# Attention block on one core: projection jobs in halves over two slots, z double-buffered and in parts, the shift copied straight to its row

## The chip, the cores and the metric

The kernel runs on one core of a Trainium2 chip. The metric is the device time of one launch in microseconds, as the median of several runs.

## The reference

Group norm over a 4 x 256 x 32 x 32 input (32 groups), attention with 4 heads of 64 channels over the 1024 positions of each image, an output projection and the residual:

```python
x_n = _group_norm(x, gn_w, gn_b)
q = _conv1x1(x_n, wq, bq); k = _conv1x1(x_n, wk, bk); v = _conv1x1(x_n, wv, bv)
q, k, v = (to_heads(q), to_heads(k), to_heads(v))
attn = jnp.einsum('bhqd,bhkd->bhqk', q, k) * hd ** (-0.5)
attn = jax.nn.softmax(attn, axis=-1)
out = jnp.einsum('bhqk,bhkd->bhqd', attn, v)
out = out.transpose(0, 1, 3, 2).reshape(bsz, c, h, wd)
return x + _conv1x1(out, wp, bp)
```

## The kernel before, in words

Every float32 factor is split into a float16 high and low part, and three products stand for one. Channels lie on two tiles of 128 partitions (index t or i), positions on two halves of 512 (index j).

**Slots.** The work is a hand-written order of 128 slots, 32 per image: an image has 8 units (a head and a half of its queries), a unit 4 slots of 256 keys. `G` counts all slots, `g` those of the image. In slot G TensorE makes the scores of G (four matmuls of 512 columns into `st[G % 2]`, lines 551 and 552), two score maxima of a unit six slots ahead (`maximum`, 529, into the banks `mxb`) and the weighed values of slot G - 4 (`weigh`, 24 matmuls of 64 or 65 columns into the bank `pv`). ScalarE reads the scores twice (739: float16 `p_hi`, 742: the full value, back into `st` in even slots and into `p32` in odd ones). The low half `p_lo` is their difference, on VectorE in even slots (830) and on GpSimd in odd ones (1023). `st` is free for slot G + 2 when that is done.

**The shift.** The softmax subtracts an upper bound of each query's score. VectorE reduces each maxima tile (806), joins the partial maxima (`join_max`, 811) at the end of the slot with G % 4 = 1; TensorE transposes the four columns in the next slot (`shift_transpose`, 536, which takes a turn in the banks `mxb`), VectorE scales the four rows (`row_out`, 818) and SyncE copies them to row 64 of `q_max` (`shift_to_row`, 369), where the scores of the unit two slots on read them.

**Jobs.** `JOBS` names, by slot, whole projections of 128 channels x 512 positions into the one bank `gen`: k, q, v of this image's second tile (i = 1) or of the next image, y (the output projection) of the image before, and two group statistics (mean, var). A k, q or y job is six matmuls of 512 columns, a v job 24 of 128 (`job` and `parts`, 480). ScalarE evicts the bank in the same slot, GpSimd makes the high and low halves of k and q in the next (997, 330), VectorE the low half of v (824). SyncE then copies the halves to the layouts of the matmuls (`dup_all`: six copies for k, six for q, each for both halves).

**z.** The normalised input of the next image: VectorE takes channel statistics (847), TensorE averages over groups (517, 519), ScalarE evicts, GpSimd works out the factors (`about_group_mean`, `norm_factors`), ScalarE makes `xin` into z (758, slots 10 and 11) and `z_hi` (763, slots 13 and 14), GpSimd `z_lo` (316, slots 14 and 15).

**Normalise** (837, 838) divides a unit's weighed values when its last `weigh` is done; the next unit's first `weigh` waits for it.

Instructions run in order on each engine and in the DMA queue of SyncE.

Of the kernel before, what the change touches and what calls it, by code (L numbers as in the profile page):

```python
# [6 lines left out]
F16 = mybir.dt.float16  # L7
ALU = mybir.AluOpType
# [4 lines left out]
def attention_block(nc, x, gn_w, gn_b, wq, bq, wk, bk, wv, bv, wp, bp, out):  # L13
# [17 lines left out]
    MXJ = 2 * QT + 1  # L31
# [19 lines left out]
    JOBS = {0: ("k", 1, 1, 0), 1: ("y", 0, 0, -1), 2: ("q", 1, 1, 0), 3: ("y", 1, 0, -1), 4: ("mean", 0, 0, 1),  # L51
# [9 lines left out]
    FIRST_IMAGE = {4: ("v", 0, 1, 0), 6: ("mean", 0, 0, 1)}  # L61


    MAX_MIDWAY = ((), (), (), (2, 3), (6, 7), (MXJ - 1,))
# [6 lines left out]
    with ctx:  # L71
# [29 lines left out]
        eps = sb("eps", [P, CT])  # L101
        first_use = sb("first_use", [P, CT])
# [5 lines left out]
        z_hi = sb("z_hi", [P, CT, HW], F16)  # L108
        z_lo = sb("z_lo", [P, CT, HW], F16)
# [14 lines left out]
        shift_row = sb("shift_row", [QT, 2, P], F16)  # L124
# [43 lines left out]
        s_mv = sem("s_mv")  # L168
        s_gmean = sem("s_gmean")
# [6 lines left out]
        s_zlo = [sem(f"s_zlo{t}") for t in range(CT)]  # L176
# [15 lines left out]
        s_dup = {n: sem(f"s_dup_{n}") for n in "kq"}  # L192
        s_first = [sem(f"s_first{h}") for h in range(2)]
        s_first_q1 = sem("s_first_q1")

        s_mx_full = sem("s_mx_full")
        s_mx_free = sem("s_mx_free")
        s_shift = sem("s_shift")
# [37 lines left out]

        def nth(i, j, b):
            return 4 * b + 2 * i + j
# [16 lines left out]
        def long_at(G):  # L255
            todo = job_at(G)
            return todo is not None and todo[0] in LONG
# [17 lines left out]
        def wait_p_lo(eng, G):  # L275
            wait(eng, s_plo_dve if lo_on_dve(G) else s_plo_pool, G // 2 + 1 + (G == TOTAL - 1))
# [37 lines left out]
        def z_low(eng, b, t):  # L314
            wait(eng, s_zhi, CT * (b - 1) + t + 1)
            eng.tensor_tensor(z_lo[:, t, :], xin[:, t, :], z_hi[:, t, :], ALU.subtract).then_inc(s_zlo[t], 1)

        def wait_z(eng, b, j=1):

            if b == 0:  # L320
                wait(eng, s_z0_lo, CT * (j + 1))
            else:
                for t in range(CT):
                    wait(eng, s_zlo[t], b)
# [773 lines left out]
```

## Time and profile before

| | us |
|---|---|
| median of 3 runs | 397.02 (396.8 to 398.1) |
| profiled execution | 398.07 |
| its span | 396.2 |
| TensorE busy | 368.2 (93%) |
| ScalarE busy | 304.6 (77%) |
| VectorE busy | 303.2 (77%) |
| GpSimd busy | 258.9 (65%) |

Slot 0 begins at 29.94 us, slot 32 at 116.70, slot 64 at 207.66, slot 96 at 299.09. A slot is found by its first L551 matmul. Matmul durations overlap, so the distance from one start to the next tells what one costs.

### The profile page before, as it was taken

The page shows a single profiled execution, that of the slowest core. Times are in us where ns is not written, and L with a number is a line of the kernel's source. Part 1 is how long each engine was busy: PE and PEld are TensorE (multiplying, and loading weights), DVE is VectorE, ACT ScalarE, POOL GpSimd, SP SyncE. Part 2 cuts the span into 40 slices and gives each one's busy share as a digit, 9 for nine tenths or more (in the row PEclk, how much of TensorE's full clock was granted, in tenths as well). Part 3 has the DMA queues.
Part 4 walks back from the last instruction along what each step waited for, and adds up shares of the span by engine and source line. Part 5 has one row for each costly group of instructions (what it writes and reads, how often), then busy time and mean ns, then how long its engine had stood idle before and what let it go on. Part 6 is the DMA issues. An engine that isn't in the chain of part 4 may idle for free.

```text
span 396.2 us, 11202 instructions
## 1 busy us (share of the span) xinstructions
PE 368.2 (93%) x4625; PEld 228.9 (58%) x4625; DVE 303.2 (77%) x528; ACT 304.6 (77%) x352; POOL 258.9 (65%) x219
## 2 busy tenths in 40 slices
PE   1998899999999999999999999999999989999977
PEld 1743566556655557456665557556665646655554
DVE  4778988868887868868877977867877776988543
ACT  1747889978787779977888779978787877788850
POOL 5045865888397865879297866869477854549730
PEclk9999999999999999999999999999999999999999
DMA  6054600345510711234510721104521541131013
GB/s 212 7 132 128 154 10 2 81 124 75 151 28 19 195 31 55 71 91 92 146 48 15 160 83 55 28 3 95 100 101 28 120 123 56 23 114 29 2 28 108
DMA packets 31019, 30.92 MB, mean 78 GB/s; under 512 B 18796, under 2 KB 21112, under 8 KB 30968
## 3 DMA queue, kind: packets, MB, share of 16 engines
q1 hardware_dynamic: 30944, 30.19, 29.7%
q8 instruction: 37, 0.61, 0.7%
q14 instruction: 14, 0.11, 0.1%
q10 hardware_dynamic: 24, 0.01, 0.0%
HBM read 9.44 MB, written 4.19 MB: 34 GB/s over the span
## 4 chain that ended last, share of the span: by engine, by line
PE 61%; DVE 18%; ACT 7%; issue 5%; DMA 3%; POOL 2%; DVEq 1%; SPq 1%; POOLq 1%
PE gen L480 15%; PE st L551 8%; PE st L552 8%; PE mx L529 8%; DVE mx L806 8%; PE pv L569 5%; DVE p_lo L830 5%; PE pv L572 5%; PE pv L571 5%; PE st L480 2%; ACT st L742 2%; DMA oT_lo<-o_lo 2%; ACT xin L758 2%; ACT p_hi L739 2%; DVEq L801 1%
## 5 line engine op out<-in xcount | busy, mean ns | idle before, releaser
L806 DVE TENSOR_REDUCE mx<-mx 128x1 f32<-128x512 f32 x256 | 170.9, 685 | 31.3 <-PE mx L529 27.9
L739 ACT ACTIVATE p_hi<-st 128x1024 f16<-128x1024 f32 x128 | 131.2, 1025 | 61.3 <-PE st L552 59.5
L1023 POOL TENSOR_TENSOR p_lo<-p,p_hi 128x1024 f16<-128x1024 f32 x63 | 134.2, 2130 | 62.1 <-ACT p L742 61.9
L569 PE MATMUL pv<-v_hi,p_hi 128*128 128x65 f16 x1024 | 105.8, 194 | 3.1 <-DVE o L838 2.6
L572 PE MATMUL pv<-v_hi,p_lo 128*128 128x65 f16 x1024 | 105.9, 194 | 0.0
L571 PE MATMUL pv<-v_lo,p_hi 128*128 128x64 f16 x1024 | 105.9, 193 | 0.0
L569 PEld LDWEIGHTS pv<-v_hi,p_hi 128*128 128x128 f16 x1024 | 94.5, 98 | 13.7 <-issue 5.6
L571 PEld LDWEIGHTS pv<-v_lo,p_hi 128*128 128x128 f16 x1024 | 93.6, 98 | 13.7
L551 PE MATMUL st<-q_twice,k_both 128*128 128x512 f16 x256 | 97.0, 379 | 4.8 <-DVE p_lo L830 3.4
L552 PE MATMUL st<-q_max,k_one 65*128 65x512 f16 x256 | 97.2, 380 | 0.0
L572 PEld LDWEIGHTS pv<-v_hi,p_lo 128*128 128x128 f16 x1024 | 93.7, 97 | 0.0
L830 DVE TENSOR_TENSOR p_lo<-st,p_hi 128x1024 f16<-128x1024 f32 x65 | 79.0, 1215 | 11.0 <-ACT st L742 11.0
L529 PE MATMUL mx<-k_both,q_twice 128*128 128x512 f16 x244 | 85.3, 379 | 0.9 <-DVE shift_row L818 0.5
L742 ACT ACTIVATE st<-st 128x1024 f32<-128x1024 f32 x65 | 66.4, 1022 | 0.0
L742 ACT ACTIVATE p<-st 128x1024 f32<-128x1024 f32 x63 | 64.2, 1019 | 0.0
L529 PEld LDWEIGHTS mx<-k_both,q_twice 128*128 128x128 f16 x244 | 24.2, 99 | 25.8 <-DVE mx L806 5.5
L551 PEld LDWEIGHTS st<-q_twice,k_both 128*128 128x128 f16 x256 | 25.2, 98 | 23.2 <-DVE p_lo L830 2.4
L552 PEld LDWEIGHTS st<-q_max,k_one 65*128 65x128 f16 x256 | 24.9, 97 | 19.2
L818 DVE TENSOR_SCALAR shift_row<-mx 4x128 f16<-4x128 f32 x32 | 8.9, 277 | 30.2 <-PE mx L536 30.2
L997 POOL CAST st_hi_k<-e_k 128x512 f16<-128x512 f32 x14 | 8.5, 610 | 28.5 <-ACT e_k L719 20.1
L330 POOL TENSOR_TENSOR st_lo_k<-e_k,st_hi_k 128x512 f16<-128x512 f32 x16 | 18.5, 1157 | 10.5 <-ACT e_k L719 8.5
L480 PE MATMUL gen<-w_hi_v,z_lo 128*128 128x128 f16 x128 | 22.2, 219 | 0.0
(166 smaller groups left out, 493.1 us busy)
## 6 DMA issues: line engine op xcount, KB each, us to landing
xres<-in_x_dram SPq DMA_DIRECT2D x4, 1024.0 KB, 5.1
q_twice<-st_hi_q SPq DMA_DIRECT2D x28, 128.0 KB, 2.4
out_dram<-y SPq DMA_DIRECT2D x14, 256.0 KB, 2.4
xin<-in_x_dram SPq DMA_DIRECT2D x6, 512.0 KB, 4.4
k_both<-st_hi_k SPq DMA_DIRECT2D x16, 128.0 KB, 2.3
k_one<-st_hi_k SPq DMA_DIRECT2D x16, 128.0 KB, 2.3
k_both<-st_lo_k SPq DMA_DIRECT2D x16, 128.0 KB, 2.3
q_max<-st_lo_q SPq DMA_DIRECT2D x14, 128.0 KB, 2.4
```

What stands on the lines that cost most here:

```text
L480: yield nc.tensor.matmul(dst, a, c, start=first and t == 0 and n == 0, stop=t == CT - 1 and n == 2, skip_group_check=True)
L529: nc.tensor.matmul(mxb[(MXJ * U + j) % 2][:, :], q_twice[:, head, q:q + P], k_both[:, head, halves(part)], start=True, stop=True).then_inc ...
L551: nc.tensor.matmul(dst, k_both[:, head, k], q_twice[:, head, q], start=True, stop=False)
L552: last = nc.tensor.matmul(dst, k_one[:, head, k], q_max[:, head, q], start=False, stop=True)
L569: nc.tensor.matmul(pv_v[:, q, :], hi, vh, start=k == 0 and q == 0, stop=False, skip_group_check=True)
L571: nc.tensor.matmul(pv_v[:, q, 0:D], hi, vl, start=False, stop=False, skip_group_check=True)
L572: last = nc.tensor.matmul(pv_v[:, q, :], lo, vh, start=False, stop=k == NK - 1, skip_group_check=True)
L739: nc.scalar.activation(p_hi[:, G % PR, :, :], scores, ACT.Exp, scale=SM_SCALE / M_SCALE)
L742: nc.scalar.activation(p_full(G), scores, ACT.Exp, scale=SM_SCALE / M_SCALE).then_inc(s_exp, 1)
L806: nc.vector.reduce_max(mx8[:, U % 2, tile, part:part + 1], mxb[(MXJ * U + j) % 2][:, :], AX.X)\
L830: nc.vector.tensor_tensor(p_lo[:, G % PR, :, :], p_full(G), p_hi[:, G % PR, :, :], ALU.subtract)\
L1023: nc.gpsimd.tensor_tensor(p_lo[:, G % PR, :, :], p_full(G), p_hi[:, G % PR, :, :], ALU.subtract)\
```

## The change

- **Jobs in halves** (`job(..., only=)`): the first half, channel tile t = 0 (for v the first two of its four key tiles), at the end of an even slot behind the second maximum; the second half in the next slot, between scores and maxima. Jobs stand at even slots alone; ScalarE evicts in the odd slot, GpSimd and VectorE take the result in the slot behind. For y, each half waits only for the transposes of its own tile.
- **z for two images** (`z_hi`, `z_lo` with an index b % 2), made in four pieces of 512 positions: z in slots 0, 2, 4, 6, `z_hi` in 8, 10, 12, 14, `z_lo` in 9, 11, 13, 15 (other slots for image 1). One v job moves to slot 30.
- **Statistics** of image b + 2 in slots 27 and 31 (`STATS`): the matmul writes four spare columns of the bank `pv` behind the weighed values, VectorE copies them behind the normalise; channel statistics in slots 20 to 26, one half at a time. For image 1 they stay jobs in `gen`, in slots 4 and 6.
- **Shift**: the transpose and `row_out` go. A query tile takes every fourth query (`tile_of`), so that partition p holds queries 4p to 4p + 3; ScalarE makes `shift` (128 x 4, float16) between its two exponentials, and SyncE copies 128 pieces of 8 bytes to the row.
- **p_lo on VectorE** in two instructions, and the scores and weighed values wait for a half. Normalise runs one slot earlier, behind `p_low` and the first `row_max`.
- **Copies on SyncE**: q per half (6 copies each, slots 5, 19, 25, 31), k in slots 3 and 22; one q group of image 0 stands ahead of the slots.

```diff
-    JOBS = {0: ("k", 1, 1, 0), 1: ("y", 0, 0, -1), 2: ("q", 1, 1, 0), 3: ("y", 1, 0, -1), 4: ("mean", 0, 0, 1),
-            7: ("var", 0, 0, 1), 8: ("y", 0, 1, -1), 9: ("y", 1, 1, -1), 10: ("v", 1, 0, 0),
-            12: ("v", 1, 1, 0), 17: ("k", 0, 0, 1), 18: ("k", 0, 1, 1), 19: ("q", 0, 0, 1),
-            20: ("q", 0, 1, 1), 23: ("v", 0, 0, 1), 25: ("v", 0, 1, 1), 27: ("k", 1, 0, 1),
-            28: ("q", 1, 0, 1)}
+    JOBS = {0: ("k", 1, 1, 0), 2: ("q", 1, 1, 0), 4: ("y", 0, 0, -1), 6: ("y", 1, 0, -1), 8: ("v", 1, 0, 0),
+            10: ("y", 0, 1, -1), 12: ("y", 1, 1, -1), 14: ("v", 1, 1, 0), 16: ("q", 0, 0, 1), 18: ("k", 0, 0, 1),
+            20: ("k", 0, 1, 1), 22: ("q", 0, 1, 1), 24: ("v", 0, 0, 1), 26: ("k", 1, 0, 1), 28: ("q", 1, 0, 1),
+            30: ("v", 0, 1, 1)}
+    STATS = {27: ("mean", 2), 31: ("var", 2)}
+    Z_FULL, FIRST_Z_FULL = (0, 2, 4, 6), (8, 9, 12, 13)
+    Z_HIGH, FIRST_Z_HIGH = (8, 10, 12, 14), (10, 11, 14, 15)
+    Z_LOW, FIRST_Z_LOW = (9, 11, 13, 15), (11, 12, 15, 17)
-    FIRST_IMAGE = {4: ("v", 0, 1, 0), 6: ("mean", 0, 0, 1)}
+    FIRST_IMAGE = {0: ("v", 0, 1, 0), 2: ("k", 1, 1, 0), 4: ("mean", 0, 0, 1), 6: ("var", 0, 0, 1), 8: ("q", 1, 1, 0),
+                   10: ("v", 1, 0, 0)}
...
+        def tile_of(half, tile):
+            return slice(half * HALF + tile, (half + 1) * HALF, QT)
...
             def shift_to_row(U):
                 _, head, half = unit(U)
-                wait(sp, s_mx_free, MXJ * (U + 1))
-                sp.dma_start(q_max[D:D + 1, head, halves(half)], shift_row[:, U % 2, :]).then_inc(s_shift_dma, 16)
+                wait(sp, s_shift, U + 1)
+                sp.dma_start(q_max[D:D + 1, head, halves(half)], shift[:, U % 2, :]).then_inc(s_shift_dma, 16)
...
+            sp.sem_inc(s_dup_q[0], 16 * 6)
+            dup_queries(1, 0, 0)
             for G in range(TOTAL):
                 slot(G)
...
+            def statistic(kind, b):
+                wait(pe, *((s_mv, b + 1) if kind == "mean" else (s_dev, b + 1)))
+                nc.tensor.matmul(pv[:, QT * PV:QT * PV + CT], group_avg[:, :], mv[:, :, 0] if kind == "mean" else dev2[:, :],
+                                 start=False, stop=True, skip_group_check=True).then_inc(s_stat, 1)
+                taken.append((s_gmean if kind == "mean" else s_gvar, b + 1))
...
             def slot(G):
                 if G < TOTAL:
                     scores(G)
+                top, old = maxima_at(G), slot_of(G - LAG)
+                begun = job_at(G - 1) if G % 2 else None
+                if begun and begun[0] in LONG:
+                    job(*begun, only=1)
                 if top:
...
                     maximum(U, n)
+                if old is not None:
+                    weigh(old)
+                if stat_at(G):
+                    statistic(*stat_at(G))
                 if top:
                     maximum(U, n + 1)
+                todo = job_at(G)
+                if todo:
+                    job(*todo, only=0 if todo[0] in LONG else None)
...
+            def row_shift(U):
+                wait(act, s_join, U + 1)
+                wait(act, s_shift_dma, 16 * (U - 1))
+                nc.scalar.activation(shift[:, U % 2, :], mx4[:, U % 2, :], ACT.Identity, bias=p_log[:, 0:1],
+                                     scale=-1.0 / M_SCALE).then_inc(s_shift, 1)
...
                 nc.scalar.activation(p_hi[:, G % PR, :, :], scores, ACT.Exp, scale=SM_SCALE / M_SCALE)
+                if G > 0 and maxima_at(G - 1) and maxima_at(G - 1)[1] == MXJ - 2:
+                    row_shift(maxima_at(G - 1)[0])
...
             for (kind, i, j), bank in zip(FIRST_JOBS, first_banks):
                 job(kind, i, j, 0, bank)
+            row_shift(0)
             job("v", 0, 0, 0)
...
             def p_low(G):
                 wait(dve, s_exp, G + 1)
-                nc.vector.tensor_tensor(p_lo[:, G % PR, :, :], p_full(G), p_hi[:, G % PR, :, :], ALU.subtract)\
-                  .then_inc(s_plo_dve, 1)
+                for c in range(CPS):
+                    nc.vector.tensor_tensor(p_lo[:, G % PR, c, :], p_full(G)[:, c, :], p_hi[:, G % PR, c, :],
+                                            ALU.subtract).then_inc(s_plo_dve, 1)
...
+                todo = job_at(G - 2) if G % 2 == 0 else None
+                if todo and todo[0] == "v":
+                    low(*todo)
+                if slot_of(G - 1) is not None and lo_on_dve(G - 1):
+                    p_low(G - 1)
+                if top:
+                    row_max(U, n)
+                if stat_at(G):
+                    statistic_full(*stat_at(G))
                 if old is not None and old % SPU == SPU - 1:
                     normalise(old // SPU)
+                if stat_at(G):
+                    statistic(*stat_at(G))
+                if g in (20, 22, 24, 26) and b + 2 < B:
+                    channel_stats(b + 2, (g - 20) // 4, ((g - 20) // 2 % 2,))
                 if top:
                     row_max(U, n + 1)
+                    if n == 2 * QT - 2:
+                        join_max(U)
+                if b == 0 and g in (2, 3):
+                    channel_stats(1, g - 2)
```

## Rows read from the trace of the kernel before

**Rows 1.** The page, part 1: busy us (share of the span), instructions.
```profile
PE 368.2 (93%) x4625; PEld 228.9 (58%) x4625; DVE 303.2 (77%) x528; ACT 304.6 (77%) x352; POOL 258.9 (65%) x219
```

**Rows 2.** Busy time in stretches: stretch, its length, each engine's busy us, then clock.
```profile
29.94:41.05 11.11, 8.61 (x39) 3.32 (x38) 9.67 (x17) 8.40 (x11) 6.50 (x7) 1.00 0.35 107
41.05:51.73 10.68, 9.99 (x149) 6.95 (x150) 9.66 (x17) 8.34 (x11) 7.32 (x8) 1.00 0.67 147
51.73:72.59 20.86, 19.89 (x297) 13.29 (x294) 17.76 (x31) 19.88 (x23) 14.18 (x15) 1.00 0.04 9
72.59:116.70 44.11, 43.76 (x569) 27.39 (x570) 35.13 (x59) 36.06 (x42) 32.55 (x26) 1.00 0.42 97
116.70:207.66 90.96, 88.63 (x1141) 55.29 (x1142) 72.42 (x123) 75.08 (x87) 66.27 (x58) 1.00 0.32 83
207.66:299.09 91.43, 88.77 (x1141) 55.22 (x1141) 72.46 (x123) 75.08 (x87) 66.29 (x58) 1.00 0.29 71
299.09:345.43 46.34, 44.55 (x568) 27.49 (x569) 34.77 (x59) 35.59 (x41) 29.22 (x21) 1.00 0.28 70
345.43:368.44 23.01, 21.68 (x303) 13.09 (x303) 20.68 (x36) 19.25 (x21) 17.03 (x9) 1.00 0.23 65
```

**Rows 3.** Waits in image 2: us in total, times, longest us.
```profile
DVE shift_row L818 <- PE mx L536: 8.4, 8, 2.2
PEld gen L480 <- DMA oT_lo<-o_lo: 1.0, 1, 1.0
```

**Rows 4.** Timeline, TensorE: slots' first score matmuls; start us, duration us, instruction.
```profile
81.86 0.38 PE L551 MATMUL st<-q_twice,k_both 128*128 128x512 f16 x1
85.19 0.38 PE L551 MATMUL st<-q_twice,k_both 128*128 128x512 f16 x1
...
110.26 0.38 PE L551 MATMUL st<-q_twice,k_both 128*128 128x512 f16 x1
112.29 0.38 PE L551 MATMUL st<-q_twice,k_both 128*128 128x512 f16 x1
114.45 0.38 PE L551 MATMUL st<-q_twice,k_both 128*128 128x512 f16 x1
```

**Rows 5.** Timeline, TensorE in image 2: a transpose, and what it waited for.
```profile
250.92 0.27 PE L536 MATMUL mx<-ident,mx 128*4 128x128 f32 x1 [0.66 <-DVE mx L811]
```

**Rows 6.** Timeline, ScalarE in slot 122; then a group of its instructions (mean ns).
```profile
369.51 1.02 ACT L739 ACTIVATE p_hi<-st 128x1024 f16<-128x1024 f32 x1
370.43 1.02 ACT L742 ACTIVATE st<-st 128x1024 f32<-128x1024 f32 x1
...
L722 ACT ACTIVATE v_hi<-gen 128x512 f16<-128x512 f32 x16 | 9.6, 601 | 1.6 <-PE gen L480 1.6
```

**Rows 7.** Timeline of the start: SyncE's queue, GpSimd and TensorE's weight load.
```profile
26.89 0.73 SPq L369 DMA_DIRECT2D q_max<-shift_row  x1
...
36.78 1.15 POOL L330 TENSOR_TENSOR st_lo_q<-e_q,st_hi_q 128x512 f16<-128x512 f32 x1
...
38.60 0.64 SPq L369 DMA_DIRECT2D q_max<-shift_row  x1
...
41.02 0.10 PEld L551 LDWEIGHTS st<-q_twice,k_both 128*128 128x128 f16 x1 [1.10 <-DMA q_max<-shift_row]
```

**Rows 8.** DMA issues by line: count, median us from issue to landing.
```profile
oT_lo<-o_lo SPq DMA_TRANSPOSE x15, 2.5
```

**Rows 9.** Timeline, GpSimd in image 1: first and last step of the factors.
```profile
142.80 0.70 POOL L980 TENSOR_TENSOR rstd<-veps,expo 128x2 f32<-128x2 f32 x1
...
145.69 0.20 POOL L990 TENSOR_TENSOR z_b<-beta_z,z_m 128x2 f32<-128x2 f32 x1
```

**Rows 10.** Timeline, TensorE: first score matmul of slot 127.
```profile
379.97 0.39 PE L551 MATMUL st<-q_twice,k_both 128*128 128x512 f16 x1 [1.03 <-POOL p_lo L1023]
```

**Rows 11.** Groups of weight loads: busy us, mean ns, idle before.
```profile
L529 PEld LDWEIGHTS mx<-k_both,q_twice 128*128 128x128 f16 x244 | 24.2, 99 | 25.8 <-DVE mx L806 5.5 <-issue 0.9 <-DVE shift_row L818 0.9
L630 PEld LDWEIGHTS pv<-group_avg,ident 128*128 128x128 f32 x12 | 2.6, 327 | 0.0
```

More of the change, by code:

```diff
@@ L175, in attention_block @@
         s_zhi = sem("s_zhi")
-        s_zlo = [sem(f"s_zlo{t}") for t in range(CT)]
+        s_zlo = sem("s_zlo")
         s_z0_32 = sem("s_z0_32")
@@ L322, in wait_z @@
             else:
-                for t in range(CT):
-                    wait(eng, s_zlo[t], b)
+                wait(eng, s_zlo, 4 * (b - 1) + CT * (j + 1))
         def low_kq(eng, kind, i, j, b):
@@ L457, in _ @@
             held = []
+            taken = []
             def bank_empty():
@@ L473, in bank_empty, with part, job @@
                     wait(pe, {"mean": s_gmean, "var": s_gvar}[kind], b + 1)
-            def parts(dst, lhs, rhs, first=True):
-                for t in range(CT):
-                    (lh, ll), (rh, rl) = lhs(t), rhs(t)
-                    for n, (a, c) in enumerate(((lh, rh), (lh, rl), (ll, rh))):
-                        yield nc.tensor.matmul(dst, a, c, start=first and t == 0 and n == 0,
-                                               stop=t == CT - 1 and n == 2, skip_group_check=True)
-            def job(kind, i, j, b, bank=gen, midway=()):
+            def part(dst, lhs, rhs, t, first=True):
+                (lh, ll), (rh, rl) = lhs(t), rhs(t)
+                for n, (a, c) in enumerate(((lh, rh), (lh, rl), (ll, rh))):
+                    last = nc.tensor.matmul(dst, a, c, start=first and t == 0 and n == 0, stop=t == CT - 1 and n == 2,
+                                            skip_group_check=True)
+                return last
+            def job(kind, i, j, b, bank=gen, only=None, midway=()):
                 if kind in "kqv":
@@ L489, in job @@
                     wait(pe, s_dev, b + 1)
-                if kind == "y":
-                    wait(pe, s_oT[j], 16 * 4 * (b + 1))
-                if bank is gen:
+                if bank is gen and only != 1:
                     bank_empty()
@@ L527, in maximum @@
                 tile, part = mx_part(U, j)
[L528 to L529 removed]
+                nc.tensor.matmul(mxb[j % 2][:, :], q_twice[:, head, tile_of(half, tile)], k_both[:, head, halves(part)],
                                  start=True, stop=True).then_inc(s_mx_full, 1)
[L532 to L536 removed]
             def scores(G):
@@ L557, in weigh @@
                 b, head, _ = unit(U)
-                wait_p_lo(pe, G)
+                if not lo_on_dve(G):
+                    wait_p_lo(pe, G)
+                if taken:
+                    wait(pe, *taken.pop())
                 if s == 0:
```

304 lines of the change are left out of this document (144 added, 160 removed).

## The prediction

> **What bounds the kernel now.** I read in this order: the page's busy shares, the same shares image by image, the waits of one steady image, and then single slots in the timeline. TensorE is busy 368.2 of 396.2 us [rows 1], no other engine more than 77%, so the end can move only by what TensorE stands still, and by work taken off it. By image [rows 2]: image 0 takes 86.76 us (its four stretches are 11.11, 10.68, 20.86 and 44.11), image 1 90.96, image 2 91.43; image 3 takes 46.34 for its first 16 slots and 23.01 for the next ten, which hold no job. The clock column is 1.00 in all of them.
>
> A slot is read from one first score matmul to the next [rows 4]. Without a job and without a wait it is 112.29 - 110.26 = 2.03 us. With a projection job it is 85.19 - 81.86 = 3.33, so a job of six wide matmuls costs 1.30, one of them 0.216; the 24 short weighing matmuls are what is left of 2.03 behind six wide ones, 0.73. The slot from 112.29 to 114.45 holds the transpose of the maxima: 2.16, so 0.13 more. A steady image has 32 slots and 16 jobs: 32 x 2.025 + 16 x 1.30 = 85.6 us of pure TensorE work (I price the v jobs, of the same number of columns, like the others), plus 8 transposes at 0.11 to 0.13, 1.0. Image 2 took 91.43: 4.8 us are standstill. Where: VectorE and TensorE wait for each other around the transpose. VectorE sits idle 8.4 us of image 2 for the transposed maxima [rows 3], and TensorE 0.66 before the transpose at 250.92 for the joined maximum [rows 5]. A y job waits 1.0 for the transposed low half [rows 3]. The rest is unevenness: two or more slots of 2.03 in a row, where ScalarE and VectorE fall behind, then slots of 3.33, where they idle.
>
> **The change, part by part, in a steady image.**
> (a) Transpose and row_out go: 8 x 0.12 = 1.0 off TensorE; VectorE loses 8 row_outs and its wait. What is late next is the shift: it now needs a ScalarE instruction in the queue between two exponentials, and one copy. Counted from the slot's first score matmul: scores done and read after 1.07; p_hi 0.92 (start to start, 369.51 to 370.43) [rows 6]; row_shift, of a shape not in the trace, 0 to 0.6 (the v eviction of 512 [rows 6] is the upper end), taken 0.2 because it has 4 elements; SyncE 0.1. So the copy is issued at 2.3. Its 128 pieces of 8 bytes aren't in the trace: the old row copy issued at 38.60 had landed when its reader went on at 41.02, so took at most 2.4 [rows 7]; a transposing copy lands in 2.5 [rows 8]. I take 2.2, range 1.6 to 3. It lands at 4.5, and the scores that need it start two slots later: at 5.36 where jobs fill the slots (slack 0.9), at 4.1 where none do (0.4 late).
> The Trainium skill, "DMA: Bandwidth & Descriptors", section Specifications, wants at least 512 B per transfer for line rate and speaks of a read-modify-write below that. That speaks against pieces of 8 B; its section "Why small descriptors are slow (HBM only)" exempts copies inside SBUF. By the first, the copy would take 3 us, which is 0.8 more in the 7 units without jobs and a gain smaller by some 5; no row here shows which holds.
> (b) Jobs in halves: each slot is 2.025 + 0.65 = 2.68 with a job in hand every second slot. ScalarE per pair of slots: 4 x 0.92 + one eviction 0.6 + one half of z 0.6 in slots 0 to 14 = 4.9 of 5.36. VectorE per pair: 4 maxima at 0.6, p_lo as two halves of 0.6 and half of a normalise 0.3, 3.9, with the statistics 0.8 more. GpSimd 2.1 + 1.8. All fit, so TensorE runs without standing still, and the waits on halves of p_lo cost nothing when they are satisfied.
> (c) y jobs come at slots 10 and 12 instead of 8 and 9: the 1.0 wait for the transposed halves goes; the copies' two slots of lead hide it.
> (d) Statistics two images ahead: one matmul at slots 27 and 31, 0.1 each, 0.2 in all. The factors chain on GpSimd runs from 142.80 to 145.89 [rows 9], 3.1 us. The statistic of slot 31 is issued at 2.5 of its slot and copied after the normalise at 3.5; factors are ready at 6.7. ScalarE wants them for z at 2.68 + 2.95 = 5.6. It stands 1.1 us, and p_hi of slot 1 starts 0.9 late; p_lo has 1.6 us until its buffer is wanted, so this costs nothing, and it is caught up within some four slots.
> Sum: 85.6 + 0.2 = 85.8, and I allow 0.7 for small waits: 86.5. Image 1 gains 90.96 - 86.5 = 4.4; image 2, 91.43 - 86.5 = 4.9.
> (e) Queue of SyncE: q copies in halves make 24 instead of 12 per image at about 0.64 each (the shift copy at 38.60 takes SyncE that long [rows 7]), 7.7 us more in a queue with half its time free. Moved past it is the shift of slot 26, which now stands behind six q copies and six k copies; I find it issued at 2.6 instead of 2.3. Slack is 0.9: nothing.
>
> **Image 3.** First 16 slots, 8 jobs: 16 x 2.025 + 8 x 1.30 = 42.8, with 0.5 of waits 43.3 against 46.34: gain 3.0. The ten slots without jobs: a pair that waits for the shift takes 4.5, the other 4.1 (p_lo in halves lets the first score matmuls start 0.6 earlier), so 8.6 per four slots, 21.4 against 23.01: gain 1.6. From there scores(127) still waits for GpSimd's p_lo of slot 125 [rows 10], which nothing moves: no gain, and none in the 16.2 us behind it.
>
> **Image 0.** Slots 0 to 3: VectorE has 8 maxima, 2 p_lo, a v low half and both channel statistics (3.4) to do, 11.3, about the 11.1 of now. But SyncE is the tighter one. Its shift copy of unit 0 was issued at 26.89; ScalarE now produces that after its last first job, some 0.95 later, and everything behind it on SyncE slides by that. Then GpSimd's k halves and q halves (36.78 + 1.15 = 37.9 now; 38.5 then [rows 7]), and six q copies, moved ahead of the slots, which wait for these: the copy of shift 1 goes from 38.60 to 41.1 and lands at 42.9 or later. Slot 4 starts at 42.9 instead of 41.05: 1.8 lost. Slots 4 to 7 hold no long job: 8.4 against 10.7, gained 2.3. Slots 8 to 15 now hold 3 jobs: TensorE 16.2 + 3.9 = 20.1, but ScalarE 8 x 1.87 (two at 0.92 and the step to the next) + 8 x 0.6 (z) + 3 x 0.6 = 21.6 and 1.1 for the factors (as in d); some 0.7 of it spills over: 22.0 against 20.9, lost 1.1. Slots 16 to 31: 16 x 2.025 + 8 x 1.30 + 0.3 = 43.1 against 44.1, gained 1.0. In all 0.4; I write 0.3.
>
> **Total**: 0.3 + 4.4 + 4.9 + 3.0 + 1.6 = 14.2. The profiled execution has a span of 396.2 and took 398.07; less 14.2 it is 383.9, or 96.4% of it. Its median over the runs is 397.02, so 382.9.
>
> **The rivals.**
> (1) The start goes smoothly too: SyncE isn't late and ScalarE catches up. Then image 0 comes near its TensorE sum, 32 x 2.025 + 13 x 1.30 - 2.9 (no weighing in four slots) = 78.8, and 0.5; gain up to 7, 376 to 380. For it: ScalarE is busy only 73 of the 86.76 us. Against: the queue order above. Chance 0.12.
> (2) A new wait in each image: ScalarE's wait for the factors, or the keys of the next image, which land only about 0.6 before the first maximum wants them at slot 26. If one of the two is 1.5 us later than I find, VectorE or TensorE pays 1 to 2 per image: 386 to 390. For it: GpSimd is in order and both hang on it. Chance 0.15.
> (3) Slower: the shift copy itself. Before slot 4U there are 3.1 us for it in slots with jobs (24 of 31 units) and 1.9 in the 7 without. At a copy of c us the change loses 24(c - 3.1) + 7(c - 1.9) and eats all of the gain, also what I have already counted, at about c = 3.3; at c = 4 it is 36 us, less the 14, so near 419. Against: nothing in rows 7 and 8 lands later than 2.5. Chance 0.05.
> (4) Slower: strided weight loads. The query tiles of the maxima are now every fourth column. A load of a query tile takes 99 ns and hides under a matmul of 216 ns; the float32 loads, read at a slower rate, take 327 [rows 11]. At that rate each would stick out by 0.11 behind a score matmul and 0.30 behind the short weighing matmuls, 0.41 a slot in 122 slots: 50 us, less the 14, so near 433; it begins to cost at about 0.2 us. Chance 0.04.
> The Trainium skill, "TensorE: Matmul & The Clock Gate", section on weight-path perf modes, says the fast weight load is kept for 128 non-float32 columns with a step up to 1,024 elements, packed or strided; by it (4) doesn't occur. No row of before has a strided 16-bit load.
> (5) The change does little, because TensorE's standstill only changes place, VectorE finding its maxima later behind p_lo: 393 to 399. Chance 0.07.
>
> **How the numbers follow.** Forecast 382.9, chance 0.57, own range 380 to 386. With (1) below and (2) above, 378 to 390 leaves out (3), (4), (5) and the edge of (1), about 2 in 10. Faster by over 0.3% (what a measurement can tell from no change): 0.57 + 0.12 + 0.15 + 0.03 of (5) = 0.87. Same 0.03. Slower 0.10: (3), (4) and the last part of (5).
>
> **What would show it.** Job slots at 2.68 each, with images 1 and 2 at 86 to 87 us; VectorE's wait for a transpose gone; ScalarE's longest wait before a z_full at slot 0, about 1 us; the copies of the shift landing within 2.5 us and scores waiting for them only in image 3 behind slot 16 and at slot 4; slot 4 of image 0 starting later than now. Wrong, if query-tile loads are longer than 0.1 us, or if the images stay above 89.

## The result and the profile after

The changed kernel takes 386.08 us (median, 385.17 to 387.66), the kernel before 397.23 beside it; the ratio is 0.972, with a 95% interval of 0.969 to 0.975. The forecast was 382.9 with a range of 378 to 390. Its profiled execution took 385.64 us, with a span of 383.9. By the medians 11.2 us are gained of the 14.1 forecast.

First the engines of the changed kernel (the page, part 1: busy us, share of the span, instructions), against [rows 1]:

```profile
PE 361.5 (94%) x4593; PEld 227.7 (59%) x4593; DVE 307.8 (80%) x565; ACT 310.7 (81%) x392; POOL 259.8 (68%) x226
```

Then its stretches, cut at the same slots as [rows 2] (stretch, length, busy us of PE, PEld, DVE, ACT, POOL, then clock):

```profile
29.57:41.20 11.63, 8.49 (x55) 4.07 (x55) 11.01 (x20) 8.89 (x11) 6.17 (x6) 1.00 0.54 154
41.20:49.72 8.52, 8.52 (x124) 5.79 (x125) 7.81 (x15) 7.02 (x10) 5.92 (x6) 1.00 0.43 94
49.72:72.08 22.36, 21.50 (x295) 13.48 (x295) 17.27 (x33) 20.67 (x29) 16.84 (x19) 1.00 0.11 23
72.08:117.76 45.68, 44.28 (x569) 27.76 (x568) 38.88 (x72) 37.62 (x48) 32.82 (x29) 1.00 0.40 96
117.76:205.24 87.48, 86.87 (x1134) 55.21 (x1133) 73.85 (x133) 76.85 (x98) 66.45 (x60) 1.00 0.34 86
205.24:291.80 86.56, 86.15 (x1130) 54.94 (x1128) 71.62 (x126) 76.60 (x97) 66.31 (x57) 1.00 0.31 75
291.80:334.76 42.96, 42.96 (x565) 27.46 (x564) 35.98 (x63) 36.21 (x45) 28.79 (x20) 1.00 0.27 63
334.76:356.34 21.58, 21.21 (x302) 13.05 (x301) 20.46 (x39) 19.50 (x24) 16.43 (x9) 1.00 0.32 93
```

Image 2 went from 91.43 to 86.56 us. TensorE's busy time in it fell by 2.6 and what it stands still from 2.7 to 0.4. Image 1 gained 3.5, the first 16 slots of image 3 gained 3.4, its next ten 1.4. Image 0 (88.19 us in its four stretches, 86.76 before) lost 1.4: slots 4 to 7 gained 2.2 and all the others lost. The prediction's 4.8 us of standstill in image 2 are 2.66 that stand idle in [rows 2] and 2.17 that the profile books as busy beyond 85.6 + 1.0.

A steady slot pair of image 2 (timeline; start us, duration, engine, instruction), for [rows 4]:

```profile
210.61 0.38 PE L571 MATMUL st<-q_twice,k_both 128*128 128x512 f16 x1
...
212.25 1.03 ACT L769 ACTIVATE p_hi<-st 128x1024 f16<-128x1024 f32 x1
213.16 0.31 ACT L762 ACTIVATE shift<-mx,p_log 128x4 f16<-128x4 f32 x1
213.29 0.38 PE L571 MATMUL st<-q_twice,k_both 128*128 128x512 f16 x1
213.34 1.04 ACT L774 ACTIVATE st<-st 128x1024 f32<-128x1024 f32 x1
213.49 0.51 SPq L385 DMA_DIRECT2D q_max<-shift  x1
...
215.97 0.38 PE L571 MATMUL st<-q_twice,k_both 128*128 128x512 f16 x1
```

213.29 - 210.61 and 215.97 - 213.29 are 2.68 each: an undisturbed slot with half a job takes that. The shift takes 0.18 of ScalarE's queue (213.16 to 213.34), and its copy is issued 2.88 us into the slot. What is left of waits in the whole run (us in total, times, longest us), and in a second view the copies (count, KB, median us from issue to landing):

```profile
PEld st L571 <- DMA q_max<-shift: 7.1, 11, 2.7
ACT xin L793 <- POOL z_b L1031: 3.5, 3, 1.7
PEld mx L555 <- DMA k_one<-st_hi_k: 2.3, 3, 1.2
```

```profile
q_max<-shift SPq DMA_DIRECT2D x32, 1.0 KB, 1.9
```

Neither a wait for a transpose nor one for `oT_lo` is among them, both of [rows 3]. New is a wait of the scores for the shift's copy, and one of the next image's first maximum for its keys (`k_one`). The copies land 1.85 to 2.1 us after issue in 27 of 32 cases, but 2.9 to 3.6 in five (issued at 80.30, 91.58, 103.85, 179.13 and 266.60). SyncE's queue around two of these, slots 22 to 26 of image 0 (the issue at 103.85 itself takes 1.50 us instead of 0.51):

```profile
91.58 0.51 SPq L385 DMA_DIRECT2D q_max<-shift  x1
92.13 2.40 SPq L396 DMA_TRANSPOSE oT_hi<-o_hi  x1
...
98.45 1.24 SPq L369 DMA_DIRECT2D k_one<-st_hi_k  x2
99.73 2.51 SPq L375 DMA_DIRECT2D q_twice<-st_hi_q  x4
102.69 1.12 SPq L379 DMA_DIRECT2D q_max<-st_lo_q  x2
103.85 1.50 SPq L385 DMA_DIRECT2D q_max<-shift  x1
```

The two `k_one` copies go out at 98.45 and the first maximum that wants them stands until 101.80:

```profile
101.80 0.41 PE L555 MATMUL mx<-k_both,q_twice 128*128 128x512 f16 x1 [0.72 <-DMA k_one<-st_hi_k]
```

### The profile page after: what moved, and what is told of

It is laid out like the page before. It is cut to its first block, busy times and chain, and to the rows that moved or that the text cites. A ratio compares the mean times of both kernels' runs of the same rounds, so it can differ in the third digit from the quotient of the medians.

```text
span 383.9 us, 11261 instructions
## 1 busy us (share of the span) xinstructions
PE 361.5 (94%) x4593; PEld 227.7 (59%) x4593; DVE 307.8 (80%) x565; ACT 310.7 (81%) x392; POOL 259.8 (68%) x226
## 4 chain that ended last, share of the span: by engine, by line
PE 66%; SPq 8%; ACT 6%; POOL 5%; issue 5%; DVE 4%; DMA 4%; POOLq 1%; DVEq 0%; ACTq 0%
PE gen L501 14%; PE st L571 10%; PE st L572 10%; PE mx L555 9%; PE pv L594 6%; PE pv L597 6%; PE pv L596 6%; POOL p_lo L1064 3%; SPq L396 3%; PE st L501 3%; DMA q_max<-shift 2%; ACT p_hi L769 2%; DVE mx L843 1%; SPq L375 1%; DMA xin<-in_x_dram 1%
## 5 line engine op out<-in xcount | busy, mean ns | idle before, releaser
L843 DVE TENSOR_REDUCE mx<-mx 128x1 f32<-128x512 f32 x256 | 173.1, 686 | 32.8 <-PE mx L555 25.7
L862 DVE TENSOR_TENSOR p_lo<-st,p_hi 128x512 f16<-128x512 f32 x130 | 83.6, 684 | 21.8 <-ACT st L774 20.3
L555 PE MATMUL mx<-k_both,q_twice 128*128 128x512 f16 x244 | 92.3, 381 | 1.7 <-DMA k_one<-st_hi_k 1.2
L555 PEld LDWEIGHTS mx<-k_both,q_twice 128*128 128x128 f16 x244 | 27.7, 114 | 18.0 <-DVE mx L843 3.0
L501 PE MATMUL gen<-w_hi_v,z_hi 128*128 128x128 f16 x128 | 23.0, 219 | 0.3 <-DVE v_lo L854 0.2
L501 PE MATMUL gen<-w_hi_v,z_lo 128*128 128x128 f16 x128 | 23.0, 219 | 0.0
```

What stands on the lines that cost most here:

```text
L501: last = nc.tensor.matmul(dst, a, c, start=first and t == 0 and n == 0, stop=t == CT - 1 and n == 2, skip_group_check=True)
L555: nc.tensor.matmul(mxb[j % 2][:, :], q_twice[:, head, tile_of(half, tile)], k_both[:, head, halves(part)], start=True, stop=True).then_inc ...
L843: nc.vector.reduce_max(mx8[:, U % 2, tile, part:part + 1], mxb[j % 2][:, :], AX.X)\
L862: nc.vector.tensor_tensor(p_lo[:, G % PR, c, :], p_full(G)[:, c, :], p_hi[:, G % PR, c, :], ALU.subtract).then_inc(s_plo_dve, 1)
```

## The experiments

All ratios are to the kernel before, run beside each of them. "The changed kernel" is the one above.

### Which part ends the standstill

**The straight shift alone**, added to the kernel before (`row_shift`, `tile_of` and the copy of 128 pieces in, `shift_transpose` and `row_out` out, jobs as before):

```diff
-                if done is not None:
-                    shift_transpose(done)
```

> The kernel before with the straight shift alone: no transpose, no row_out, ScalarE makes the shift, query tiles of every fourth query, copy of 128 pieces. Theory: TensorE loses 31 transposes at 0.12 us (3.7) and VectorE its wait for them, worth another 1 to 3: 390.5 to 393. Rival: the copy's pieces and the place between two exponentials cost what the transposes gave, above all in slots without jobs: 395 to 398. Slots without a job around the shift tell: 2.03 to 2.2 by the theory.

396.62 us, ratio 0.998 (0.997 to 0.999): it gains 0.7 to 0.8, and the rival held. Images 1 and 2 take 91.28 and 90.94. Slots 78 to 80 of image 2, timeline:

```profile
248.83 0.38 PE L546 MATMUL st<-q_twice,k_both 128*128 128x512 f16 x1
...
250.86 0.38 PE L546 MATMUL st<-q_twice,k_both 128*128 128x512 f16 x1
...
251.55 0.31 ACT L731 ACTIVATE shift<-mx,p_log 128x4 f16<-128x4 f32 x1
251.74 1.03 ACT L743 ACTIVATE st<-st 128x1024 f32<-128x1024 f32 x1
...
252.80 1.23 DVE L826 TENSOR_TENSOR p_lo<-st,p_hi 128x1024 f16<-128x1024 f32 x1 [0.97 <-ACT st L743]
...
254.14 0.10 PEld L546 LDWEIGHTS st<-q_twice,k_both 128*128 128x128 f16 x1 [1.22 <-DMA q_max<-shift]
254.17 0.38 PE L546 MATMUL st<-q_twice,k_both 128*128 128x512 f16 x1 [1.13 <-DVE p_lo L826]
```

The slot that held the transpose fell from 2.95 to 2.03 us (248.83 to 250.86), and the next one grew from 2.21 to 3.31. There TensorE has run ahead into slots without a job: the second exponential ends at 252.77, p_lo at 254.03, and the next scores wait 1.13 for the bank that p_lo reads. The shift's copy, issued at 251.88, lands at 253.76, only 0.3 before p_lo ends, so it would be the next to hold them. The standstill moved by one slot.

**The old transposing shift, put back into the changed kernel** (jobs in halves, z, statistics and y stay):

```diff
+                if shift_at(G) is not None:
+                    shift_transpose(shift_at(G))
                 if top:
```

> The changed kernel with the shift of the kernel before: TensorE transposes the joined maxima, VectorE writes them out as a row of four parts, one copy from there; contiguous query tiles; jobs, z, statistics and y as in the changed kernel. The straight shift alone, added to the kernel before, gave 0.8 us. Theory (the evenly spaced halves of jobs end the standstill, and the transpose costs its own 0.12 us and a short wait for the joined maximum at each of 31 shifts): slots with a transpose take 2.8 to 3.1 instead of 2.68, images 1 and 2 take 88 to 90 us, the kernel 389 to 393. Rival, what the prediction held (TensorE and VectorE wait for each other around the transpose, whatever the jobs do): images 1 and 2 stay near 91 and the kernel at 395 or above. A third outcome, that the transpose costs nothing in even slots, would be 386 to 388.

396.07 us (394.92 to 399.88), ratio 0.999 (0.996 to 1.001). Neither theory had it: the images are as the first said, at 90.11 and 89.68, but the sum over 31 shifts and the start is larger than its 389 to 393 (no stretch but slots 0 to 3 and 16 to 31 is as short as in the changed kernel), and nearly the whole gain is gone. A slot with the transpose takes 3.16 instead of 2.68 (timeline, TensorE and then VectorE):

```profile
225.62 0.38 PE L580 MATMUL st<-q_max,k_one 65*128 65x512 f16 x1
226.20 0.27 PE L564 MATMUL mx<-ident,mx 128*4 128x128 f32 x1 [0.20 <-DVE mx L849]
226.31 0.38 PE L557 MATMUL mx<-k_both,q_twice 128*128 128x512 f16 x1
...
225.17 0.69 DVE L844 TENSOR_REDUCE mx<-mx 128x1 f32<-128x512 f32 x1 [0.24 <-PE mx L557]
225.90 0.16 DVE L849 TENSOR_REDUCE mx<-mx 128x4 f32<-128x8 f32 x1
```

The group of all transposes (busy us, mean ns, idle before):

```profile
L564 PE MATMUL mx<-ident,mx 128*4 128x128 f32 x32 | 8.6, 269 | 8.9 <-DVE mx L849 8.9
```

The last score matmul starts at 225.62 and one is worth 0.22, so TensorE could go on at 225.84; VectorE's joined maximum comes out at 226.06 and the transpose starts at 226.20, 0.36 late. The transpose itself is 0.11 (to 226.31). 0.36 + 0.11 is the 0.48, and eight of them are 3.8 us an image. Images 1 and 2 are only 2.6 and 3.1 longer than in the changed kernel, since the late keys and copies of the shift at its slots 55, 58 and 91 are missing here. So the shift alone is worth 0.7 to 0.8 us, everything else alone at most 1.1 (its interval includes no gain), and both together 11.2. That each takes away what the other would still be late for is how I read this; the rows above show one late wait in each of the two runs.

**Half a job ahead of that transpose**, as a whole job stood there in the kernel before (the edit is to the run just above):

```diff
+                todo = job_at(G)
+                early = shift_at(G) is not None and todo and todo[0] in LONG
+                if early:
+                    job(*todo, only=0)
                 if shift_at(G) is not None:
                     shift_transpose(shift_at(G))
```

> The last run put the old transposing shift back into the changed kernel and came to 396.1 us, so that the whole gain went. There each slot with a transpose takes 3.16 us instead of 2.68: TensorE has finished its scores 0.36 us before VectorE has the joined maximum, and the transpose itself takes 0.11. Here the first half of the slot's job, 0.65 us, which stood at the end of the slot, goes in front of the transpose, as whole jobs did in the kernel before. Theory (the 0.36 is a matter of order and hides behind the half job; only the 0.11 are the transpose's own): slots with a transpose take 2.75 to 2.85, images 1 and 2 87.0 to 88, the kernel 387 to 390. Rival (the maxima fall behind the transpose: VectorE gets the first maximum of the next unit 0.65 later, and its weighed values and the next scores with it): these slots still take over 3 us and the kernel 394 to 397.

398.01 us, ratio 1.002 (1.001 to 1.004), images 90.93 and 90.42 (in the profiled execution the clock was at its lower level for 6.8 us, but only from 380.45, in slot 127 and behind it). The theory fell, though not by the rival's mechanism, and the time is above the rival's range too. In image 2 five of the eight slots with a transpose take 2.90 to 3.00, the others 3.67 to 3.80. Two rows, of slots 66 and 70:

```profile
218.12 0.38 PE L499 MATMUL gen<-z_hi,w_hi_q 128*128 128x512 f16 x1 [0.85 <-ACT e_k L756]
...
229.02 0.10 PEld L499 LDWEIGHTS gen<-oT_hi,w_hi_p 128*128 128x128 f16 x1 [0.43 <-ACT y L764]
```

The job's bank `gen` is still being evicted: 0.85 of waiting in slot 66, which takes 3.80, and less in slot 70, which takes 2.90. Neither of the two places tried for the transpose is free of a wait.

**Whole jobs, one every second slot**, the rest as changed:

```diff
-                if begun and begun[0] in LONG:
-                    job(*begun, only=1)
...
-                    job(*todo, only=0 if todo[0] in LONG else None)
+                    job(*todo)
```

> The changed kernel with each job whole at the end of its even slot instead of in halves over two slots; all else as changed. If halving is what removes the standstill, slots of 2.03 and 3.33 us alternate and images 1 and 2 lose 3 us or more each: 393 or above. If the even distance of the jobs (one every second slot) is enough, because p_lo has 1.6 us of slack, the pairs of slots stay at 5.36 us and the time within 1.5 us of the changed kernel, 385 to 387.5. I take the second as likelier, 2 to 1.

388.27 us (388.24 to 388.36), ratio 0.977 (0.976 to 0.978). Slots alternate between 3.33 and 2.03, and images 1 and 2 take 88.46 and 87.39, 1.0 and 0.8 more than in halves. The time lies between the two expectations, nearer the second. So cutting the jobs in two is worth about 2 us, and most of the gain stays without it. That the even distance of the jobs carries the rest is argued: z in parts, the statistics, the early normalise and the halves of p_lo changed with it, and z, statistics and normalise weren't tried apart.

### Parts that were costed at nothing or little

**p_lo in one instruction** instead of two halves, with one wait:

```diff
-                for c in range(CPS):
-                    nc.vector.tensor_tensor(p_lo[:, G % PR, c, :], p_full(G)[:, c, :], p_hi[:, G % PR, c, :],
+                nc.vector.tensor_tensor(p_lo[:, G % PR, :, :], p_full(G), p_hi[:, G % PR, :, :],
```

> The changed kernel with p_lo on VectorE in one instruction again, and whole waits. Theory: nothing in slots with jobs; in the ten slots of image 3 without jobs a pair takes 0.3 to 0.6 us more, 1.5 to 3 in all, and about 0.5 in slots 4 to 13 of image 0: the kernel takes 387.5 to 389.5. Rival: the halves hide nothing because VectorE loses a start per slot, 0.06 x 64: the kernel takes 385.5 or less.

387.51 us (385.61 to 387.83), ratio 0.974 (0.971 to 0.977): not to be told from the changed kernel. Three of its four executions have a mean clock of 0.995 or 0.996 (see the last section); the one at full clock took 385.61. By stretch there is a difference, smaller than the theory's 1.5 to 3: the ten slots without jobs take 22.18 instead of 21.58 and slots 122 to 126 take 11.72 instead of 11.33, as less of p_lo is done when the scores want its bank; images 1 and 2 take 86.67 and 86.12, 0.8 and 0.4 less, which is within what they differ by between traces (see the order of SyncE's queue below). A gain of the halves shows only where no job fills the slot.

**Adjacent queries** in each query tile instead of every fourth one, so that the weight loads aren't strided; `P_LOG` is 0, and the queries get each other's shifts, so the softmax subtracts other values than it should and the output isn't the reference's:

```diff
-            return slice(half * HALF + tile, (half + 1) * HALF, QT)
+            return slice(half * HALF + tile * P, half * HALF + (tile + 1) * P)
```

> The changed kernel with query tiles of 128 adjacent columns, so the weight loads of the maxima aren't strided; the shift then goes to the wrong queries and its constant is 0, so the output isn't the reference's, while all instructions and waits stay. Loads go back from 113 to 99 ns. Theory: hidden, same time within 0.3%. Rival: the 14 ns stick out behind the short matmuls in 122 slots, up to 1.7 us: 384.4.

385.94 us, ratio 0.971 (0.969 to 0.974), image 1 at 87.32 and image 2 at 86.92: the strided loads cost nothing that shows. In the changed kernel a load of a query tile takes 114 ns against 99 [rows 11], hidden under matmuls of 216:

```profile
L555 PEld LDWEIGHTS mx<-k_both,q_twice 128*128 128x128 f16 x244 | 27.7, 114 | 18.0 <-DVE mx L843 3.0 <-DMA k_one<-st_hi_k 2.3 <-issue 1.4
```

**y jobs early again**: the y jobs of the second half in slots 8 and 10, v in 12 and 14.

```diff
-            10: ("y", 0, 1, -1), 12: ("y", 1, 1, -1), 14: ("v", 1, 1, 0), 16: ("q", 0, 0, 1), 18: ("k", 0, 0, 1),
+            10: ("y", 1, 1, -1), 12: ("v", 1, 0, 0), 14: ("v", 1, 1, 0), 16: ("q", 0, 0, 1), 18: ("k", 0, 0, 1),
```

> The changed kernel with the y jobs of the second half in slots 8 and 10, as near to the transposing copies of slot 6 as in the kernel before, and the v jobs in 12 and 14. Theory (the later place is what ended the 1.0 us wait for the transposed low half): TensorE or its weight load waits 0.7 to 1.5 us in slot 8 of images 1 to 3 and the kernel takes 388 to 390 us. Rival (a y job in halves waits only for its first half of channels and finds it there): no such wait, 385.5 to 386.8.

386.91 us (383.98 to 389.19), ratio 0.973 (0.968 to 0.978). No wait for a transposed half is in its trace, and images 1 and 2 take 87.06 and 86.64. The rival held, though the median is 0.1 above its range: the 1.0 of [rows 3] doesn't come back with the early place. The profiled execution is the slowest, for another reason. In image 0 the edit leaves slot 10 without a job, slot 12 waits 1.69 for the copy of the shift, and the clock is at its lower level twice, for 3.4 us each.

### What is still lost, and a faster version

**SyncE's queue at the start.** In the changed kernel slot 4 waits for the copy of shift 1, which stands behind six q copies. Here three of them, not needed before slot 8, go behind it:

```diff
+                if G == 3:
+                    dup_queries(1, 0, 0)
...
-            dup_queries(1, 0, 0)
```

> Slot 4 of image 0 starts at 41.2 us in the changed kernel, where TensorE waits 2.2 us for the copy of shift 1, which SyncE issues at 39.18 behind six q copies (35.5 to 39.1). Here the three of them that head 1 needs only from slot 8 on are issued in slot 3, behind that shift copy. Theory (SyncE's order sets the start of slot 4): the copy is issued some 1.8 us earlier, slot 4 starts at 39.4 to 39.8 and all behind it moves along: 384.2 to 384.6 us against 386.1. Rival (something else is due at the same point, the joined maximum, the weighed values or a clock that is not full yet): slot 4 starts after 40.8 and the time stays at 385.7 to 386.4. Images 1 to 3 don't change in either.

384.58 us, ratio 0.970 (0.967 to 0.973). Before slot 4 in the changed kernel, and the same place and the end of slot 4 here:

```profile
41.20 0.39 PE L571 MATMUL st<-q_twice,k_both 128*128 128x512 f16 x1 [2.19 <-DMA q_max<-shift]
```

```profile
40.33 0.38 PE L572 MATMUL st<-q_twice,k_both 128*128 128x512 f16 x1 [0.65 <-DVE p_lo L863]
...
43.68 0.38 PE L537 MATMUL gen<-mv,group_avg 128*128 128x2 f32 x2 [0.90 <-DVE mv L882]
```

Slots 0 to 3 are 1.46 us shorter (10.17), as the theory has it, and slots 4 to 7 are 1.42 longer (9.94): now VectorE's channel statistics are awaited. Slot 8 starts as late after slot 0 as it did, 20.1 us. So the 1.5 by which the median is lower isn't this edit's own path. Both profiled executions have the full clock and differ by 0.6, and image 1, which the edit doesn't touch, is 1.1 shorter here (86.38); the executions at full clock overlap, 383.92 to 385.86 here and 385.17 to 386.52 in the changed kernel.

**SyncE's order in the images**: the transposing copies a slot later, both input loads in one slot, the q copies of slot 25 in slot 27, behind the shift of slot 26.

```diff
-                done = output_at(G - 1)
+                done = output_at(G - (1 if G >= TOTAL - 2 else 2))
...
-                    if g == 25:
+                    if g == 27:
                         dup_queries(0, 1, b + 1)
```

> In the changed kernel SyncE issues a transposing copy in slots 6, 14, 22, 30 just behind the copy of a shift, then both input loads in slots 17 and 18, and the six q copies of slot 25 ahead of the shift of slot 26. The shift copies beside them land in 2.9 to 3.6 us instead of 1.9, and slots 19, 26, 27, 55, 58, 59 and 91 are 0.3 to 0.7 us longer. Here the transposing copies are issued a slot later (behind no shift copy), both loads in one slot, and the q copies in slot 27, behind the shift. Theory (SyncE's order and what is in flight delays the shift copies and the next keys): these slots go back to 2.68, images 0 to 2 gain 0.7 to 1.5 us each, in all 3 to 3.5: 382.6 to 383.6 us. Rival (the copies are slow whenever any transfer is in flight, and the stall only moves to slots 28 and 31 or to the waits for transposed halves in the y jobs): 385.3 to 386.5.

384.65 us, ratio 0.969 (0.965 to 0.972), where 382.6 to 383.6 was expected. The profiled execution, slots 4 to 7 and then slots 16 to 31 of image 0 and images 1 and 2:

```profile
41.60:51.72 10.12, 10.12 (x125) 6.86 (x126) 8.01 (x15) 7.02 (x10) 5.90 (x6) 0.83 0.36 79
...
74.06:118.57 44.51, 43.92 (x569) 27.81 (x568) 38.66 (x72) 37.60 (x48) 32.55 (x29) 1.00 0.38 99
118.57:204.96 86.39, 86.39 (x1134) 55.35 (x1133) 73.65 (x133) 76.82 (x98) 66.51 (x60) 1.00 0.34 87
204.96:290.92 85.96, 85.96 (x1129) 54.99 (x1128) 71.62 (x126) 76.59 (x97) 66.33 (x57) 1.00 0.31 75
```

The last three stretches gain 1.2, 1.1 and 0.6 against the changed kernel's trace, 2.9 together, just under the 3 to 3.5 expected; slots 26, 55, 58 and 91 are back at 2.68, slot 19 isn't (3.23, its copy of the shift lands 3.6 us after issue, as before). In images 1 and 2 TensorE's busy time is the whole stretch. 1.6 of the gain went at once, in slots 4 to 7, where the clock is 0.83. But 2.9 is the difference of two single executions, and the old order differs from one to the next: with it image 1 takes 87.48, 86.67, 87.32, 86.38, 86.80 and 87.06 us in the changed kernel and the runs with whole p_lo, adjacent queries, the new start, later z and early y. The three stretches average 45.43, 86.95 and 86.63 over these six traces, and 44.75, 86.38 and 86.05 over the three with the new order. By that the order is worth about 1.8 us, an estimate from these averages.

**The first z piece a slot later**, so that ScalarE doesn't wait 1.7 for the factors in slot 8:

```diff
-    Z_FULL, FIRST_Z_FULL = (0, 2, 4, 6), (8, 9, 12, 13)
+    Z_FULL, FIRST_Z_FULL = (0, 2, 4, 6), (9, 10, 12, 13)
```

> In slot 8 of image 0 ScalarE waits 1.7 us for the factors of the normalisation, and slots 8 to 15 take 22.36 us. Here ScalarE's first z piece is one slot later (pieces in slots 9, 10, 12, 13 instead of 8, 9, 12, 13, with their high and low parts moved likewise). Theory (ScalarE, standing still, is what lengthens slots 8 to 15): they take 21.2 to 21.6 us, the kernel 385.0 to 385.4. Rival (ScalarE had slack there, and the slots are set by VectorE or by the shift of slot 12): 22.2 to 22.5 and no change, 385.8 to 386.4.

386.11 us (383.65 to 387.5), ratio 0.973 (0.969 to 0.977): no gain in the median, but slots 8 to 15 take 21.54 instead of 22.36, as the theory has it, and slots 4 to 7 take 10.14, at the same lower clock as in the run above. Three of the four executions are like that; the one at full clock took 383.65.

**The three together:**

> The three edits together: q copies of head 1 behind the shift in slot 3, the transposing copies a slot later with the q copies of the next image behind the shift of slot 26, and the first z piece a slot later. If the stalls are separate the gains add up, 1.7 + 3.3 + 0.9 = 5.9, which gives 380.2 us (379.5 to 381.5). If an early start only makes the later slots of image 0 wait for GpSimd's or VectorE's work on the next image, the first of the three is lost again: 381.5 to 383.

382.80 us (381.88 to 383.08), ratio 0.965 (0.963 to 0.967), so the gains don't add up to 380.2 and the second expectation held. It is faster than the changed kernel by 3.3, about what slots 8 to 31 (0.8 and 0.9) and images 1 and 2 (1.1 and 0.6) give; the first edit's own gain is given back in slot 4.

**And the mean of image 1 behind the weighing of slot 5**, where it doesn't hold the scores back:

```diff
+                if begun and begun[0] == "mean":
+                    job(*begun)
```

> The three edits of the last call together, and TensorE's matmul of the mean of image 1 moved from the end of slot 4 to behind the weighing of slot 5. With the three alone slot 4 takes 3.59 us, of them 1.4 in front of that matmul, which waits for VectorE's channel statistics until 43.9 us. Theory (TensorE is held only because that matmul stands in its queue ahead of the next scores): slots 4 to 7 take 8.5 to 8.9 instead of 9.94 and the kernel 381.5 to 381.9, against 382.8. Rival (VectorE itself is late there, with its maxima behind the same statistics): slot 4 or 5 still takes over 3 us and the time stays at 382.5 to 383.

382.53 us (381.94 to 382.61), ratio 0.962 (0.960 to 0.964). Slot 4 takes 2.29 instead of 3.59, slot 5 takes 3.01 instead of 2.02: its first maximum waits 0.58 for VectorE, and the mean now stands in it. 0.3 is gained of 1.3, so the rival held: VectorE is what is late there. This is the fastest version, 3.5 us under the changed kernel.

## Why the prediction was right, and where it wasn't

The forecast span was 396.2 - 14.2 = 382.0, measured 383.9. The median, 386.08, lies in the range of 378 to 390 and just outside the narrower 380 to 386. Of the 1.9 missing in the span, image 0 has 1.7 and image 1 has 1.0; image 3 and the two ends give about 0.7 back, and the rest is rounding. Its steps:

- **The slot.** 2.68 with half a job was forecast; measured 2.67 to 2.71 in nearly all of them. Images 1 and 2: forecast 86.5, measured 87.48 and 86.56. Image 3: 43.3 and 21.4 forecast, 42.96 and 21.58 measured, and 0.2 gained behind it where nothing was forecast. This is what made the sum right: it was built from TensorE's own work in a slot, and not from the waits that would go.
- **(a) The shift.** The copy takes 1.9 us (taken 2.2, range 1.6 to 3), with the five exceptions above. ScalarE's part is 0.18 (taken 0.2). The issue was put at 2.3 into the slot and is at 2.88, because the first exponential starts 1.64 into the slot and not at 1.07: ScalarE is still busy evicting the job. So the copy lands at 4.8 and the slack is 0.6, not 0.9. With so little slack scores also wait for a late copy where jobs fill the slots (slots 20, 56 and 92), and not only at slot 4 and in image 3, as was said under what would show it.
- **The standstill.** The text put it down to VectorE and TensorE waiting for each other around the transpose, and the rest to unevenness, as if the two were parts of a sum. The runs with one part each show a condition on both: at most 0.8 and 1.1 us alone, 11.2 together. Rival (5), that the standstill only changes place, is what the shift alone does.
- **(b)** Waits for the halves of p_lo cost nothing, as said. Halves against whole jobs are worth 2 us; that the even distance is the rest is argued.
- **(c)** The y wait went, but its reason, two slots of lead, wasn't it: with early y jobs it stays away. Whether the wait per half or the smoother slots end it wasn't tried.
- **(d)** ScalarE waits 0.9 for the factors in images 1 and 2 (forecast 1.1), and it costs nothing there. The statistics were put at 0.1 each; slots 27 and 31 take 2.90 and 2.91 even where nothing waits, so 0.22 each. The profile shows two float32 weight loads for each (0.19 one, 0.30 from the first start to the last end) and two matmuls; that the loads are what sticks out is argued.
- **(e) failed.** "Nothing" was said of the queue of SyncE. The order of its queue costs 2.9 us in images 0 to 2 between the two traces, and about 1.8 on the average of nine, by late keys and late copies of the shift. This is half of rival (2), the keys that land close to the first maximum, and a part that no rival had: a 1 KB copy that lands 1.0 to 1.7 us later where larger transfers go with it.
- **Image 0.** Forecast 86.5, measured 88.19, by two misses of opposite sign, so it is partly luck that the sum came so near. The start was put too late: the copy of shift 1 goes out at 39.18 and not 41.1, since GpSimd's q half is ready sooner, and slot 4 starts at 41.20 instead of 42.9. And slots 16 to 31, forecast 43.1, take 45.68: slots 16 (0.55, for VectorE's `v_lo` and `o`), 19 (0.56), 26 (0.92), 27 (0.46) and 31 (0.23) are longer than 2.68. ScalarE's wait in slot 8 was 1.7, not 1.1, and worth 0.8.
- **Rivals (3) and (4)**, both slower: the copy stays under its limit of 3.3 but for two landings, and the strided load is 114 ns where 200 would begin to cost. One sign of being wrong in the prediction, loads of a query tile longer than 0.1 us, did come true at 114 ns. That sign was set too low, by the prediction's own 0.2: packed loads of 99 ns give the same time within the noise. Nor was its 327 ns what a float32 load always takes: those of the statistics take 219 in the mean in the trace before and 190 here. The Trainium skill, "DMA: Bandwidth & Descriptors", section Specifications, would have made the copy of 8 B pieces slower, and its section "Why small descriptors are slow (HBM only)" not; the trace agrees with the second, with 1.9 us for 128 pieces beside 2.1 for the 64 KB copies into `q_twice`. The first gives no time; the 3 us that the prediction puts beside it are the upper end of its own range. The Trainium skill, "TensorE: Matmul & The Clock Gate", section "Weight-path perf modes", keeps the fast load for strided columns; 114 against 99 ns agrees nearly.

## What to carry to other kernels

Where one engine is the bound, add up its own work per step and forecast from that sum, then look for the chain that is late next; removing one of two waits can gain next to nothing (here 0.8 us), so test the parts of such a change together and alone. Spread extra work evenly, in pieces as small as the step allows, since every step then has some slack for a chain of exponential, low half and shift. One profile isn't enough for a difference of 1 us: image 1 took 87.48 and 86.38 in two kernels that are alike in it. A small copy on a queue isn't small for who waits for it: look at what is issued just behind it and what is in flight.

## What the hardware showed that I had not expected

**TensorE's clock in slot 4.** In six of the kernels (the changed one and those with whole p_lo, adjacent queries, another order on SyncE, a later z and early y) TensorE stands still for about 2.2 us before slot 4. In 14 of their 24 executions the mean granted clock is 0.99 to 0.996, in the others at least 0.999. With whole jobs it stands still for 1.56 there, and in none of the 4 executions is the clock below 0.999. In the three whose start queue was changed it is 0.65, and in none of 12 is the clock below 0.999. The profile of the run with another order on SyncE shows where:

```profile
39.00:41.60 2.60, 0.42 (x3) 0.01 (x1) 2.53 (x6) 1.89 (x3) 0.84 (x2) 1.00 0.35 71
41.60:43.50 1.90, 1.90 (x8) 0.81 (x9) 1.61 (x4) 0.33 (x1) 1.79 (x2) 0.61 0.32 69
43.50:45.40 1.90, 1.90 (x29) 1.81 (x28) 0.76 (x2) 1.61 (x2) 1.45 (x1) 0.50 0.64 145
45.40:47.40 2.00, 2.00 (x31) 1.30 (x32) 2.00 (x4) 0.95 (x2) 0.00 (x0) 1.00 0.83 189
```

Right behind the standstill the clock is at its lower level, 1.2 instead of 2.4 GHz, for 3.4 us; slot 4 takes 3.78 us instead of the 2.18 of the changed kernel's profile, which stood still as long and kept its clock. Of the executions with another order on SyncE, the one at full clock took 382.96 and those below 384.58 to 384.99. So a standstill of 2.2 us goes with a lower clock in over half of the executions, and one such fall costs 1.6 us. This weighs on the medians above: another order on SyncE, whole p_lo, later z and early y each have three of four executions with a lower mean clock, the changed kernel one.

It isn't only slot 4. With early y the clock fell once more, at 65.99, 2.0 us after TensorE had stood still for 1.69 before slot 12. In the run with half a job ahead of the transpose it fell at 380.45, right behind 1.59 us of standstill before slot 127, for 6.8 us. The 1.40 us before slot 127 that nine of the traces have is in none of them followed by a fall within 10 us. What decides whether it falls stays open.

**A 1 KB copy in company.** 128 pieces of 8 bytes land after 1.9 us. With the two input loads or a row of key, query or transposing copies around them, it is 2.7 to 3.8 us, in the changed kernel and in the three that change SyncE's order in the images, and moving the transposing copies away doesn't change it (3.6 and 2.8 in slots 18 and 22 of image 0). Which of the companions delays it stays open.
